# Reordering one tile's top-k steps on VectorE in a fused transformer kernel

## What is computed

```python
# layer 0, per batch
h = _self_attn(_ln(x) * (1 + sc) + sh)        # 16 heads of 16, windows of 128 tokens, rolled by 64
x = x + h * g_msa
# cross attention to 64 context tokens, the 16 best scores of each row alone
scores = einsum('bqhd,bkhd->bhqk', q, k) / sqrt(D)
top_s, top_i = jax.lax.top_k(scores, 16)
attn = softmax(top_s); o = sum of attn * v[top_i]
x = x + (o @ w_co + b_co) * g_mca
x = x + swiglu(_ln(x) * (1 + sc) + sh) * g_mlp
# layer 1: adaptive layer norm, full cross attention to 64 rows, projection
x = x + (softmax(q3 k / sqrt(D)) v @ Wp + bp)
```

## Time and profile before

| what | value |
|---|---|
| median of 3 runs | 1108.52 us (1107.9 to 1109.76) |
| the profiled execution | 1104.54 us, span 1102.7 us |
| TensorE busy | 935.9 us, 85% of the span |
| VectorE busy | 784.7 us, 71% |
| ScalarE busy | 472.2 us, 43% |
| GpSimd busy | 208.0 us, 19% |
| TensorE's mean granted clock | 0.93 of full speed |

### The profile page before, as it was taken

The page is one execution under the profiler, slowest core; times in us unless marked ns, Lnnn a source line. Parts: engine busy times, 40 slices in busy tenths (PEclk is TensorE's granted clock), DMA queues, the critical chain, the costliest instruction groups (busy, mean ns, idle before and its releaser), DMA issues.

```text
span 1102.7 us, 23080 instructions
## 1 busy us (share of the span) xinstructions
PE 935.9 (85%) x8080; PEld 679.5 (62%) x8080; DVE 784.7 (71%) x3968; ACT 472.2 (43%) x789; POOL 208.0 (19%) x159
## 2 busy tenths in 40 slices
PE   4986816899899989899999988998999897967975
PEld 4764515578567765577568755786667654744753
DVE  5154696699759975799579964997699757874212
ACT  0133413472646255553565263635563555314312
POOL 0010312230114030411041220401041302110110
PEclk8689857999999999899999998999999999989898
DMA  8360000100010012000010102100100110000000
GB/s 307 130 240 21 10 1 2 40 30 2 2 53 1 1 50 84 21 11 1 15 41 1 49 2 84 30 1 2 40 15 1 50 44 1 1 1 20 1 1 20
DMA packets 29475, 39.36 MB, mean 36 GB/s; under 512 B 4512, under 2 KB 25120, under 8 KB 28848
## 3 DMA queue, kind: packets, MB, share of 16 engines
q1 hardware_dynamic: 29360, 37.85, 10.3%
HBM read 28.34 MB, written 9.50 MB: 34 GB/s over the span
## 4 chain that ended last, share of the span: by engine, by line
PE 50%; DVE 32%; issue 8%; ACT 6%; DMA 2%; SPq 1%; POOL 1%; DVEq 0%; ACTq 0%; POOLq 0%
PE bank L1180 48%; DVE left L1047 9%; DVE top L1045 8%; DVE negm L1011 4%; DVE xh L891 3%; DVE negm L1076 2%; PE bank L1253 2%; DVE arena L1069 2%; ACT arena L778 2%; ACT arena L804 1%; DMA qk<-in_rows 1%; DVE x L973 1%; DVE arena L1038 1%; DVE vpad L1002 1%; DMA out<-x 1%
## 5 line engine op out<-in xcount | busy, mean ns | idle before, releaser
L1180 PE MATMUL bank<-w_m,arena 128*128 128x256 f32 x512 | 114.7, 385 | 2.4 <-issue 2.4
L595 POOL TENSOR_SCALAR veps<-mv 128x4 f32<-128x4 f32 (+1 forms) x33 | 7.9, 240 | 561.7 <-DVE mv L886 561.7
L1180 PEld LDWEIGHTS bank<-w_m,arena 128*128 128x128 f32 x512 | 98.2, 193 | 17.5 <-issue 3.7
L635 POOL TENSOR_TENSOR eS<-arena,top 128x1024 f32<-128x1024 f32 x32 | 61.9, 1934 | 223.5 <-DVE top L1045 223.5
L1047 DVE MATCH_REPLACE8 left<-top,arena 128x64 f32<-128x64 f32 x512 | 100.0, 215 | 0.0
L1047 DVE MATCH_REPLACE8 left<-top,left 128x64 f32<-128x64 f32 x512 | 100.0, 214 | 0.0
L759 ACT ACTIVATE arena<-bank 128x512 f32<-128x512 f32 x128 | 66.1, 603 | 69.3 <-PE bank L1180 69.3
L794 ACT ACTIVATE rden<-bank,chan 128x512 f32<-128x512 f32 x64 | 44.0, 688 | 103.1 <-PE bank L1180 82.4
L1180 PE MATMUL bank<-qr,w_m 128*128 128x512 f32 x256 | 83.3, 406 | 1.3 <-ACT qr L719 1.1
L1011 DVE TENSOR_REDUCE negm<-bank 128x4 f32<-128x512 f32 x128 | 78.7, 688 | 6.6 <-PE bank L1180 6.6
L1180 PE MATMUL bank<-qr,m_low 128*128 128x512 f32 x256 | 80.9, 398 | 0.0
(11 more groups left out here) (116 smaller groups left out, 1905.5 us busy)
## 6 DMA issues: line engine op xcount, KB each, us to landing
w_m<-in_w_m SPq DMA_DIRECT2D x4, 1024.0 KB, 5.2
kbd<-keys_by_head SPq DMA_DIRECT2D x8, 512.0 KB, 3.4
arena<-in_w_ada SPq DMA_DIRECT2D x1, 2304.0 KB
xin<-in_x SPq DMA_DIRECT2D x4, 512.0 KB, 4.1
arena<-in_w_m SPq DMA_DIRECT2D x1, 2048.0 KB, 10.3
out<-x SPq DMA_DIRECT2D x4, 512.0 KB, 2.9
gate<-gate_rows SPq DMA_DIRECT2D x12, 128.0 KB, 3.5
gated_bias<-gate_rows SPq DMA_DIRECT2D x12, 128.0 KB, 3.7
```

Source lines behind the costliest of these rows:

```text
L635: nc.gpsimd.tensor_tensor(eS[:], S[:, t, :].rearrange("p (h n) -> p h n", h=H), top[:, :, 0:1].to_broadcast([P, H, LC]), ALU.subtract).the ...
L1180: return nc.tensor.matmul(dst, lhsT, rhs, start=start, stop=stop)
```

## The change

Three steps of the fourth tile's top-k change places with window divisions on VectorE. The second MAX8 (step 2) goes from behind `last_max` to in front of the second division, and the second removal and the product (steps 3 and 4) go from behind the third division to in front of it.

```diff
-                topk(3, (1,))
+                topk(3, (1, 2))
                 if front:
                     window_divide(1)
                 if back:
                     last_max(0)
                     last_max(1)
-                topk(3, (2,))
+                topk(3, (3, 4))
                 if front:
                     window_divide(2)
-                topk(3, (3, 4))
                 if back:
                     cross_divide(4)
```

## The result

The changed kernel took 1125.14 us (median of 4 runs, 1120.67 to 1126.53) against 1109.14 us before in the same comparison: ratio 1.0133, 95% interval 1.0095 to 1.0171. (The ratios in this text are estimates from the single runs of both kernels and not the quotient of the medians, which is 1.0144 here.) The forecast was 1122. Measured again, in a later comparison, it took 1126.17 us, ratio 1.0159 (1.0128 to 1.0190).

The account below looks back on a forecast made before the run. TensorE and ScalarE together were taken to set the end of each rolled half. Stall +11.4, clock +4.7 and fill -2.2 gave +13.9 us: 1118.4 on the profiled scale, 1122 on that of the medians, range 1115.2 to 1127.

Parts of the forecast that it names:

- the stall: Six rolled halves: TensorE's last_products(1) starts 1.9 us later in each, +11.4 us (10.7 to 11.8).
- MAX8 into the gap costs nothing: Rolled halves, before the second division: the moved MAX8 step fits VectorE's wait with 2.2 us to spare, cost nothing.
- The third division 2.33 us later: Rolled halves, VectorE: behind removal and product the third division starts at 654.12, not 651.79.
- It holds the bank of last_products(1): Rolled halves: last_products(1) can't start before the third division drains the PSUM bank it takes next in rotation.
- Hand-over 0.10 to 0.27 us, no slack, 1.9 us a half: Rolled halves: TensorE starts that long after the third division ends, and ScalarE's second four exps move by the whole 1.9.
- VectorE's earlier end is worth nothing in the rolled halves: Rolled halves: the 2.03 us VectorE gains is worth nothing, since cross_divide waits for ScalarE.
- The clock, +4.7, bounds 0 to 7.0: Rolled halves, L799 to first residual: the longer pause lowers TensorE's clock in four more halves, 1.17 us each.
- the case with two pieces: Rival, rolled halves: the clock falls twice a half, another 7.0 us, 1129.4 us in all; chance 0.07.
- The fill, -2.2, bounds -1.8 to -4.0: Fill's second half: removal and product move into VectorE's wait, so the fourth division and project(1) come 2.2 us earlier.
- The drain, nothing: Drain's first half: MAX8 fits the 2.71 us gap and cross_divide waits 1.49 us for ScalarE, so no change.

Follow-up runs that it names:

- the other bank assignment: Third window's PV key two places later in the bank list, with the changed VectorE order and with the old one: ratios 1.0056 and 1.0063 against the kernel before.
- the wide filler: Changed kernel plus two useless matmul calls on all 128 rows while TensorE waits for the third division: 1106.20 us, ratio 0.9976 against the kernel before.
- the fill alone: Changed order only in halves without back, old order in rolled halves and drain; timed twice against the kernel before: ratios 0.9988 and 0.9959.
- that with the product behind: Changed kernel, but the product goes back behind the third division while the removal stays in front: 1106.01 us, ratio 0.9985 against the kernel before.
- both with fillers in the stall: Changed kernel plus two useless matmul calls before last_products(1), on 32 rows or on the whole array: ratios 1.0055 and 0.9976 against the kernel before.
- the two with the short filler: Changed order in the fill only, plus one 256-column whole-array matmul before last_products(1): ratio 0.9915; with two more matmuls in each drain half: 0.9895; against the kernel before.

## Why the prediction was right, step by step

The forecast had 1122 (1115 to 1127), slower; measured were 1125.1 and 1126.2. The mechanism was right. Of the sum 11.4 + 4.7 - 2.2 = 13.9 us the profile shows 10.8 + 7.6 - 3.9 = 14.5, so the stall was nearly right in size, while the clock's cost and the fill's gain were both taken too small, and these two errors nearly cancel: that is in part luck. So is that the profiled spans differ by 16.2 and no more, since two things that the sum did not have, +5.2 in the drain and -6.0 at the start, cancel too.

- *MAX8 into the gap costs nothing.* Shown: 2.14 us of the gap remain (2.2 forecast), and that step alone gives 1.0007 and leaves all six stages at 11.02 us.
- *The third division 2.33 us later.* It starts 3.21 us after L799 in place of 0.89: 2.32.
- *It holds the bank of last_products(1).* Shown twice: by the releaser in the row at 293.11, and by the other bank assignment, under which both orders take the same time.
- *Hand-over 0.10 to 0.27 us, no slack, 1.9 us a half.* Hand-over 292.86 to 293.11, 0.25 us. The group starts 3.88 us after L799 in place of 1.91, 1.97 later, and at full clock the stage grows by 1.80: there is some 0.17 us of slack, and the term is 10.8 us and not 11.4.
- *VectorE's earlier end is worth nothing in the rolled halves.* The kernel in which the MAX8 alone moves has it, and its stages take 11.02 as before.
- *The clock, +4.7, bounds 0 to 7.0.* Right in kind, too small, and in the profiled execution just past its upper bound. Before, the granted clock fell from 1.00 to 0.50 for 3.4 us in two halves (the stretches begin at 416.6 and 887.7), 0.1 to 0.2 us after TensorE had started again behind the pause of 0.77 us; the four others have pauses of 0.76 to 0.78 us in this place and stay at 1.00. That a longer pause would bring the fall in all four was thus an estimate from two halves, and no run shows the 4 x 1.17. The changed kernel has 0.50 in all six, for 3.4 us in four and for 6.8 in two. Six stages at 12.82 would sum to 76.9; the profiled execution has 86.90, so the clock takes 10.0 there, against 2.4 before: +7.6. The repeat has +6.6. The term was sized as one piece of 1.17 us in four halves. But a half that loses a piece (3.4 us at 0.50) now loses 1.3 us (14.15 - 12.82), and two of the six lose 2.2 to 2.4 (15.0 to 15.2), as the case with two pieces had it.
- *The fill, -2.2, bounds -1.8 to -4.0.* Measured -3.9. project(1) starts at 188.70 in an execution that runs 6.0 us early, so at 194.7 on the scale of before, as forecast: that is the 2.2. It then ran for 3.69 us at a granted clock of 1.00 and not for 5.38 at 0.68, and this 1.7 was in the bounds but not in the sum. In the profile before, it followed the pause of 4.10 us.
- *The drain, nothing.* The order there costs nothing that a row shows, but its two stages took 5.2 us more, at a mean granted clock of 0.69 and 0.73 in place of 0.98 and 1.00. The changed order isn't the cause by itself: the kernels with the old order in the drain (the fill alone, both times) have 13.2 and 13.4 us too, and with the MAX8 alone 13.3 and 13.4. The kernel before, that with the product behind and both with fillers in the stall have 10.7 and 11.1. What of the difference between the medians is this is open; that the drain's clock depends on when the kernel arrives there is argued, not shown.

What ties the clock to TensorE's idle time is the pair of kernels with and without the wide filler: same stall, 76.93 against 85.90 us in the six stages, in one profile each. The two slower halves of the kernel before say less on this than the prediction made of them, since their pauses (0.69 and 0.77 us) are no longer than those of the four at full clock (0.69 and 0.76 to 0.78).

## What to carry to other kernels

An instruction that nobody needs soon may still hold a buffer. Before something is put in front of it, look up who takes that buffer next in the rotation, and when. Price a stall on TensorE at its own length plus what the clock does in and behind it: here 10.8 us of stall went with 6.6 to 7.6 us of clock in the same stages. And where a wait on TensorE can't be removed, try work on the whole array inside it: here 1.98 us of it in each wait of 2.7 us went with 9.0 us less in the six stages, in one profile each.

## What the runs showed of the hardware

- Two useless matmuls of 128 x 512 on the whole array in a pause of 2.7 us (1.98 us of work) went with six of six stages at full clock; two of the same 512 columns on 32 rows (1.87 us of work) with three of six; none with none of six, in two profiles. The first two are one profile each.
- One of 256 columns on the whole array, in a pause of 0.76 us, went with six of six at full clock in two profiles; two profiles of the same kernel without it show one and two stages at lower clock. This is suggestive and not more: the kernel in which the MAX8 alone moves has six of six without any filler. The kernel with the filler is 0.85% faster than before, for 0.35% worked out from the fill.
- The drain's two stages take some 10.7 and 11.1 us in some profiles and some 13.3 and 13.4 in others, with the same instructions but for the fillers. The two kernels with fillers in the stall, the last filler some 100 us earlier, show the first, and so do the kernel before and the one with the product behind; five others show the second. Three lie between, one stage low and one higher: before's order on the other banks (11.23 and 12.40) and the two with the short filler (12.30 and 11.10, 10.75 and 12.26). What decides is open.
